# Resident second matrices for the first experts, a direct path for the first queries, and a masked row maximum on VectorE

## The chip, the cores and the metric

The kernel runs on one core of a Trainium2 chip. The metric is the device time of one execution in microseconds (us). TensorE (PE in the rows; PEld is its weight load) multiplies, VectorE (DVE) and ScalarE (ACT) work elementwise, GpSimd (POOL) helps and issues indirect DMAs, and SyncE (SP) issues most of the DMAs. A "q" behind an engine's name (SPq, PEldq) means its sequencer.

## What is computed

Two transformer layers over x, shaped (8, 256, 256), float32. Each has a cross attention and a mixture of experts, and each adds to x:

```python
x = x + L0_xattn(layernorm(x), ctx, ctx, mask, Wq, Wk, Wv, Wout, b_out, causal=1)
x = x + L0_ffn(layernorm(x))     # 16 experts, top 2, 256 -> 512 -> 256, relu
x = x + L1_xattn(layernorm(x), ctx, ctx, Wq, bq, Wk, bk, Wv, bv, Wo, bo)
x = x + L1_ffn(layernorm(x))     # 7 experts, top 2, capacity 732, silu gate, 256 -> 1024 -> 256, one shared expert
```

Both attentions have 16 heads of 16 channels. In the first one a score is closed (minus infinity) above the diagonal and where the mask says so, and a row with every score closed gives zero:

```python
scores = einsum('bhqd,bhkd->bhqk', q, k) / sqrt(16)
scores = where(triu(ones, k=1), -inf, scores)
scores = where(mask[:, None], -inf, scores)
attn = nan_to_zero(softmax(scores))
out = einsum('bhqk,bhkd->bhqd', attn, v)
```

## The kernel before

The work goes stage by stage: first attention, router, first experts, second attention, router, second experts. Semaphores order the engines inside a stage, and all engines meet at a stage's end.

**Attention** (`attend_block`, for both layers). A batch is one of the 8 sequences of 256 rows. Its 16 heads go in four groups of four (G = 4, NG = 4). Queries and keys are cut into three bfloat16 parts each (`split`, lines 320 to 337), whose products are stacked along the contraction dimension in `qs` and `ks`: six rows of 16 channels, so 96 of 104 partitions. To get from a channel-major tile (`parts`) to a stack (16 partitions, heads side by side) the parts go through DRAM: `store_parts` writes them, `load_stack` (lines 133 to 139) reads six pieces. For the first batch's queries `first_queries` (lines 455 to 464) stores each of the three parts as soon as it is cut, and then loads the pieces. All of that is on SP's queue, ahead of the rest of x, `wo`, the third context and the second batch's stacks.

The softmax needs each row's maximum first. `score` (lines 972 to 987) makes scores query-major, `reduce` on VectorE (lines 635 to 639) takes the maxima of a unit, `tops` cuts them in two bfloat16 parts, `turn_tops` turns them, and ScalarE copies them as extra rows into the stack `qs` (line 882). Then `scoreT` makes the scores again, key-major and with the maximum subtracted by the stack's extra rows, ScalarE takes the exponential (line 892), `value` multiplies with the values, and `normalize` divides by the row sums. In the first attention a closed score gets -1e30 added by a second product of the identity with the tile `shut` (lines 986 and 1018). A unit (`UNITS`, line 253) is a PSUM bank full of scores: in the first attention three units per group, one of four heads by 128 keys and two of two heads by 256 keys; two banks take turns (RING = 2), so a unit's scores wait for the reduction of the unit but one before it.

The order on each engine is written out by hand. On TensorE one group is (lines 1110 to 1128): scores of the next group's first unit, turn of this group's maxima, values of the group before, second unit, transposed score of head 0, head 1, third unit, turn of the outputs, heads 2 and 3; between them, by slot (lines 248 to 250), the projections of the batch two ahead and the output projection of the batch before. Batches 6 and 7 have no batch two ahead, so their groups have no such projections. VectorE's group is: the three reductions of the next group, its tops, and the normalization of the group before; in a batch's fourth group also the residual and the statistics of the batch before, and in the first batch the cut of the second queries, the statistics of x and the extra rows of the keys. VectorE's batches run in a loop (`batches`, lines 286 to 293).

**Router** (`route_block`). Norm, logits, top 2 and the lists of which rows go to which expert, mostly on VectorE. In the first layer SP loads the biases `b1` and `b2`, stores the rows and then issues ten loads for the second attention (lines 1262 to 1270).

**First experts** (`experts0_block`). The chosen rows are packed into 47 blocks of 128 rows, each of one expert. For each block SP reads the expert's number and loads both of its matrices (1,024 floats per partition each, 1 MB together) into a ring of four; block n's load waits for block n - 4 to be done. GpSimd gathers the rows, TensorE turns them (`turn`), makes the hidden layer (`first`, line 1713) and the result (`second`, line 1722), ScalarE applies relu, VectorE adds the second bias. TensorE's order is first(j + 1), turn(j + 2), second(j), eleven rounds of four in a loop and three left over.

## Time and profile before

| | us |
|---|---|
| median of 3 runs | 1268.6 (1268.25 to 1268.67) |
| span of the profiled execution | 1262.1 |
| left over for what lies around the span | 6.5 |
| TensorE busy | 1123.7 (89%) |
| VectorE busy | 690.8 (55%) |
| ScalarE busy | 595.9 (47%) |
| GpSimd busy | 360.7 (29%) |

The profiled execution has no time of its own beside its span; the median of the three runs stands for it. The stages lie in the span as follows: first attention 0 to 228 us, router to 262, first experts to about 467, second attention to about 711, router to 736, second experts to the end. Busy time is the union of an engine's instructions; matmuls are pipelined, so a matmul's duration (0.22 us, say) is longer than the step from one to the next (0.06 us), and the starts tell the pace. An idle time in square brackets stands before the row's first instruction, with what ended it. The granted TensorE clock is given as a share of 2.4 GHz.

### The profile page before, as it was taken

The numbers are of one execution on the slowest core, as the hardware profiler recorded it, in microseconds if no ns is written. First come the engines' busy times: TensorE is split into PE (matmuls) and PEld (weight loads), VectorE is DVE, ScalarE is ACT, GpSimd is POOL, SyncE is SP. The second block draws the span as 40 slices with busy tenths as digits, with TensorE's granted clock in tenths as the row PEclk, the third lists the DMA queues.
The fourth block names the chain that finished last, engine by engine and source line by source line (L and its number), as shares of the span: only waits on it lengthen the run. The fifth ranks groups of instructions, "written<-read, shape, count | busy, mean of one in ns | idle before, by whom it ended". The sixth has DMA issues, their size and how long they took to land. (4 is left out here: it accounts for less than half of the span.)

```text
span 1262.1 us, 25941 instructions
## 1 busy us (share of the span) xinstructions
PE 1123.7 (89%) x8539; PEld 974.6 (77%) x8539; DVE 690.8 (55%) x1558; ACT 595.9 (47%) x1211; POOL 360.7 (29%) x502
## 2 busy tenths in 40 slices
PE   5999998739999984888998679999999999999997
PEld 4788786329888873555665379999999999999996
DVE  4755666652222226676767655555556555555556
ACT  3566666313222222776787334444445444444432
POOL 6566650112222205776630145000000000000261
PEclk8899999859999996999999879999999999999999
DMA  7774461548999957568471221223232232232132
GB/s 182 175 180 120 129 179 37 193 159 292 332 330 325 314 207 163 111 136 146 89 125 24 100 89 59 79 63 112 72 103 76 87 109 87 86 100 73 50 97 80
DMA packets 88137, 172.56 MB, mean 137 GB/s; under 512 B 11251, under 2 KB 59949, under 8 KB 81792
## 3 DMA queue, kind: packets, MB, share of 16 engines
q1 hardware_dynamic: 71712, 136.15, 39.0%
q0 software_dynamic: 9584, 29.32, 7.9%
q10 hardware_dynamic: 6768, 6.16, 1.4%
q8 instruction: 40, 0.66, 0.2%
q14 instruction: 33, 0.27, 0.1%
HBM read 133.11 MB, written 39.20 MB: 137 GB/s over the span
## 5 line engine op out<-in xcount | busy, mean ns | idle before, releaser
L2136 PE MATMUL e_ps<-xT_e,wp_e 128*128 128x384 f32 (+1 forms) x1344 | 245.2, 331 | 4.0 <-DVE wp_e L2010 4.0
L2136 PEld LDWEIGHTS e_ps<-xT_e,wp_e 128*128 128x128 f32 x1344 | 221.7, 188 | 5.4 <-issue 4.1
L639 DVE TENSOR_REDUCE att_ps<-att_ps 128x2 f32<-128x512 f32 (+1 forms) x224 | 155.3, 697 | 103.5 <-PE att_ps L986 63.2
L1968 ACT ACTIVATE act_a_e<-e_ps 128x256 f32<-128x256 f32 (+2 forms) x176 | 77.8, 442 | 159.9 <-PE e_ps L2136 150.9
L2066 DVE TENSOR_TENSOR hid_e<-act_a_e,e_ps 128x256 f32<-128x256 f32 (+2 forms) x176 | 87.0, 494 | 116.6 <-ACT act_a_e L1968 102.4
L892 ACT ACTIVATE probs<-att_ps 128x384 f32<-128x384 f32 (+1 forms) x256 | 130.4, 546 | 41.4 <-PE att_ps L1018 29.0
L1972 ACT ACTIVATE hidp_e<-hid_e 128x256 fp32r<-128x256 f32 (+2 forms) x176 | 83.8, 476 | 127.3 <-DVE hid_e L2066 121.5
L2153 PE MATMUL e_ps<-wp_e,hidp_e 128*128 128x256 f32 (+1 forms) x1008 | 138.4, 282 | 2.9 <-DVE xres L2026 1.2
L2068 DVE TENSOR_TENSOR hidp_e<-hid_e,hidp_e 128x256 fp32r<-128x256 f32 (+2 forms) x176 | 87.8, 499 | 95.5 <-ACT hidp_e L1972 90.1
L2153 PEld LDWEIGHTS e_ps<-wp_e,hidp_e 128*128 128x128 f32 (+1 forms) x1008 | 130.7, 183 | 4.9 <-issue 4.1
L1608 ACT ACTIVATE hid_e<-e_ps,b_ahead 128x128 f32<-128x128 f32 x188 | 53.7, 368 | 139.9 <-PE e_ps L1713 129.2
L1919 POOL DMA_DIRECT2D done<-y_e x7 | 6.2, 893 | 384.3 <-DVE y_e L2050 384.3
L984 PE MATMUL att_ps<-ks,qs 96*128 96x256 bf16 (+1 forms) x512 | 102.4, 267 | 11.4 <-DMA qs<-parts 9.5
L2136 PE MATMUL e_ps<-xT_e,swp_e 128*128 128x256 f32 x768 | 106.0, 289 | 1.5 <-issue 0.8
L1016 PE MATMUL att_ps<-qs,ks 104*128 104x256 bf16 (+1 forms) x512 | 99.7, 262 | 3.4 <-ACT qs L882 1.5
L1713 PEld LDWEIGHTS e_ps<-xT_e,w_e 128*128 128x128 f32 x752 | 89.9, 194 | 16.5 <-issue 15.3
L2136 PEld LDWEIGHTS e_ps<-xT_e,swp_e 128*128 128x128 f32 x768 | 98.5, 195 | 2.8 <-DVE swp_e L2005 2.3
L1713 PE MATMUL e_ps<-xT_e,w_e 128*128 128x128 f32 x752 | 94.4, 279 | 6.4 <-DMA w_e<-in_W 5.8
L1589 POOL DMA_INDIRECT x_e<-rows,owner_e x47 | 44.7, 952 | 168.7 <-PE e_ps L1703 125.1
L882 ACT ACTIVATE qs<-att_ps 8x1024 bf16<-8x1024 f32 x64 | 65.1, 1017 | 52.9 <-PE att_ps L997 52.0
L1722 PE MATMUL e_ps<-w_e,hid_e 128*128 128x256 f32 x376 | 88.9, 380 | 0.0
L984 PEld LDWEIGHTS att_ps<-ks,qs 96*128 96x128 bf16 x512 | 48.0, 100 | 39.7 <-issue 20.7
(235 smaller groups left out, 1850.0 us busy)
## 6 DMA issues: line engine op xcount, KB each, us to landing
w_e<-in_W SPq DMA_DIRECT2D x47, 1024.0 KB
w_e<-in_W SPq DMA_DIRECT2D x57, 384.0 KB, 3.1
ks<-parts SPq DMA_DIRECT2D x96, 128.0 KB, 4.7
qs<-parts SPq DMA_DIRECT2D x96, 128.0 KB, 5.2
parts<-cut SPq DMA_DIRECT2D x30, 384.0 KB, 3.2
x_e<-rows SPq DMA_DIRECT2D x8, 768.0 KB, 5.6
done<-y_e ACTq DMA_DIRECT2D x47, 128.0 KB
rows<-zeros POOLq DMA_DIRECT2D x8, 736.5 KB, 6.6
```

Source lines behind the costliest of these rows:

```text
L639: dve.tensor_reduce(tops_at(at[3])[:, qt, x0:x0 + heads], src, AX.X, ALU.max).then_inc(reduced, 1)
L892: act.activation(probs[:, g % 2, x0, 0:WIDE], ps[:, TB + x0 % RING, 0:WIDE], ACT.Exp, scale=DK ** -0.5).then_inc(exped, 1)
L984: last = pe.matmul(out, qs[0:KS, j, hd, qt * P:(qt + 1) * P], ks[0:KS, j, hd, 0:keys(qt)], start=True, stop=not causal)
L1016: last = pe.matmul(out, ks[:, j, hd, kt * P:(kt + 1) * P], qs[:, j, hd, q0:S], start=True, stop=not causal)
L1713: last = pe.matmul(ps[:, HB + j % 2, f * P:(f + 1) * P], w1(j, c, f), xT[:, j % 2, c, :], start=c == 0, stop=c == DC - 1)
L1722: last = pe.matmul(ps[:, YB + j % 2, 0:D], hid[:, j % 2, f, :], w2(j, f), start=f == 0, stop=f == FC0 - 1)
L1968: act.activation(act_a[:, u % 2, 0:n], ps[:, AB + u % 2, 0:n], ACT.Silu).then_inc(silu_ready, 1)
L1972: act.activation(hidp[:, u % 2, 0, 0:n], hid[:, u % 2, 0:n], ACT.Copy).then_inc(hid_high, 1)
L2066: dve.tensor_tensor(hid[:, u % 2, 0:n], act_a[:, u % 2, 0:n], ps[:, BB + u % 2, 0:n], ALU.mult).then_inc(mixed, 1)
L2068: dve.tensor_tensor(hidp[:, u % 2, 1, 0:n], hid[:, u % 2, 0:n], hidp[:, u % 2, 0, 0:n].bitcast(F32), ALU.subtract).then_inc(hid_cut, 1)
L2136: last = pe.matmul(ps[:, bank + u % 2, 0:n], weights(lot, c, pw)[:, (b * DC + d) * P:(b * DC + d + 1) * P], xT[:, px, d, t0:t0 + n], start ...
L2153: last = pe.matmul(out, hidp[:, u % 2, px, t * P:t * P + rows], weights(lot, c, pw)[:, 2 * DC * P:], start=c == 0 and q == 0 and tile % 2 ...
```

## The change

1. First experts: the second matrices of all 16 experts are loaded once, into a tile `w2` of 64 KB per partition, in four loads issued in the router stage. A block's load brings the first matrix alone. TensorE reads the expert's number for each block and takes its second matrix by it. The ten loads for the second attention move from the router stage to the experts' stage, between the loads of blocks 43 and 44.
2. Both attentions: the first batch's queries go from `parts` straight into the stack, in twelve pieces of 64 KB, six issued by SP and six by ScalarE.
3. First attention: `score` leaves out the mask products. `reduce` adds the mask and takes the maximum for each head in one instruction (eight per group), writes the closed scores to a scratch tile and the maxima to SBUF instead of PSUM. VectorE's batches are written out instead of looped. The wait for `shut` moves from `score` to `reduce` and `scoreT`.

```diff
@@ first queries
+        def first_queries(eng, c):
+            for part in range(PARTS):
+                eng.wait_ge(piece_ready if part < PARTS - 1 else parts_ready[0], part + 1 if part < PARTS - 1 else 1)
+                for r in range(len(STACK_Q)):
+                    if STACK_Q[r] == part:
+                        eng.dma_start(qs[r * DK:(r + 1) * DK, 0, c * HPC:(c + 1) * HPC], parts[:, 0, KINDS.index(0), part, c]).then_inc(first_loaded[c], 16)
...
             store_and_load(0, 0, 1)
-            first_queries()
+            first_queries(sp, 0)
...
+            for loaded in first_loaded:
+                sp.wait_ge(loaded, 16 * len(STACK_Q))
+            lead(sp, parts_stored[0], 16)
+            lead(sp, stacks_loaded[0], 16 * len(STACK_Q))
...
                 take_whole(f, f, 0)
+                if f == 0 and ye is not None:
+                    first_queries(act, 1)
                 if f == 0:
                     square_root(1, 1 if ye is not None else NORM - 1, 2)
+                if f == 0 and ye is None:
+                    first_queries(act, 1)
                 if ye is None:
                     take_values(f)
@@ masked maxima
+        row_tops = sb("row_tops", [P, 2, TPB, G])
+            closed_scores = sb("closed_scores", [P, TPB, G, S], BF16)
...
-            return ps[:, MB, (g % 2) * TPB * G:(g % 2 + 1) * TPB * G].rearrange("p (t x) -> p t x", t=TPB)
+            return row_tops[:, g % 2]
...
                 dve.wait_ge(scored, ready(group(at) * NU + u))
+                if causal:
+                    if at[3] == 0 and u == 0:
+                        dve.wait_ge(shut_ready, at[0] + 1)
+                    for x1 in range(heads):
+                        col = x1 * 512 // heads
+                        last = dve.tensor_tensor_reduce(out=closed_scores[:, qt, x0 + x1, 0:keys(qt)], in0=ps[:, unit_bank(at, u), col:col + keys(qt)],
+                                                        in1=shut[:, 0, at[0], qt, 0:keys(qt)], scale=1.0, scalar=MASKED, op0=ALU.add, op1=ALU.max,
+                                                        accum_out=tops_at(at[3])[:, qt, x0 + x1:x0 + x1 + 1])
+                    last.then_inc(reduced, 1)
+                    return
...
-            batches(dve, batch)
+            if causal:
+                for n in range(B):
+                    batch(n, n % 2, n // 2, n == 0, n == B - 1)
+            else:
+                batches(dve, batch)
...
                 if g == 0 and u == 0:
-                    pe.wait_ge(stacks_loaded[j], 16 * len(STACK_Q) * 2 * (r + 1))
-                    if causal:
-                        pe.wait_ge(shut_ready, n + 1)
+                    if isinstance(n, int) and n == 0:
+                        pe.wait_ge(stacks_loaded[j], 16 * len(STACK_K))
+                        for loaded in first_loaded:
+                            pe.wait_ge(loaded, 16 * len(STACK_Q))
+                    else:
+                        pe.wait_ge(stacks_loaded[j], 16 * len(STACK_Q) * 2 * (r + 1))
...
-                    last = pe.matmul(out, qs[0:KS, j, hd, qt * P:(qt + 1) * P], ks[0:KS, j, hd, 0:keys(qt)], start=True, stop=not causal)
-                    if causal:
-                        last = pe.matmul(out, m["identb"][:], closed(n, 0, qt, 0, keys(qt)), start=False, stop=True)
+                    last = pe.matmul(out, qs[0:KS, j, hd, qt * P:(qt + 1) * P], ks[0:KS, j, hd, 0:keys(qt)], start=True, stop=True)
...
+                if x0 == 0 and g == 0 and causal:
+                    pe.wait_ge(shut_ready, n + 1)
@@ first experts
-W0 = DC * F0 + FC0 * D
+W0 = DC * F0
+W2_LOADS = 4
...
-                loaded = ahead["loaded"]
-                for name in ("Wk", "Wv", "Wq", "Wo"):
...
+                w2_sb, w2_loaded = w2
+                for e in range(0, E0, E0 // W2_LOADS):
+                    some = slice(e, e + E0 // W2_LOADS)
+                    sp.dma_start(w2_sb[:, some], a["W2_0"][:, some]).then_inc(w2_loaded, 16)
...
-        def w2(j, f):
-            return w[:, j, DC * F0 + f * D:DC * F0 + (f + 1) * D]
+        def w2(e, f):
+            return w2_sb[:, bass.ds(e, 1), f * D:(f + 1) * D].rearrange("p a d -> p (a d)")
...
-                sp.dma_start(w[:, j], a["W_0"][bass.ds(e, 1)].rearrange("a p f -> p (a f)")).then_inc(w_loaded[j], 16)
+                sp.dma_start(w[:, j], a["W1_0"][bass.ds(e, 1)].rearrange("a p f -> p (a f)")).then_inc(w_loaded[j], 16)
...
             with sp.Fori(0, ROUNDS) as i:
                 for j in range(RING):
                     load(i, j)
+            loaded = ahead["loaded"]
+            for name in ("Wk", "Wv", "Wq", "Wo"):
...
             for j in range(LEFT):
                 load(ROUNDS, j)
...
+            def expert(i, j):
+                return pe.value_load(m["block_expert"][0:1, bass.ds(RING * i + j, 1)], min_val=0, max_val=E0 - 1)
+
-            def second(i, j):
+            def second(i, j, e):
...
                 for j in range(min(known, RING)):
+                    e = expert(i, j)
                     if j + 1 < known:
                         first(*at(i, j + 1))
                     if j + 2 < known:
                         turn(*at(i, j + 2))
-                    second(i, j)
+                    second(i, j, e)
...
             first(0, 0)
+            pe.wait_ge(w2_loaded, 16 * W2_LOADS)
             with pe.Fori(0, ROUNDS) as i:
```

## Rows read from the trace of the kernel before

**Rows 1.** Table of windows; columns: busy (count) per engine, granted clock, DMA share, GB/s.
```profile
31.00:58.00 27.00, 25.50 (x230) 19.23 (x228) 20.85 (x62) 14.37 (x27) 11.86 (x29) 0.86 0.81 186
58.00:180.00 122.00, 121.31 (x1250) 98.54 (x1249) 70.24 (x190) 82.74 (x156) 78.01 (x73) 1.00 0.57 141
...
285.00:461.00 176.00, 169.59 (x1146) 152.80 (x1145) 37.40 (x88) 50.31 (x176) 37.93 (x41) 1.00 0.93 319
```

**Rows 2.** Turns of the maxima (line 997), 58 to 182 us: two per group.
```profile
L997 PE MATMUL att_ps<-identb,top_parts x42: 219/219/220, 58.8 to 180.4; 128*8 128x128 bf16 x42
```

**Rows 3.** Timeline of TensorE, first experts: the first product of four blocks.
```profile
289.11 1.95 PE L1713 MATMUL e_ps<-xT_e,w_e 128*128 128x128 f32 x16
...
292.84 1.95 PE L1713 MATMUL e_ps<-xT_e,w_e 128*128 128x128 f32 x16
...
304.84 2.02 PE L1713 MATMUL e_ps<-xT_e,w_e 128*128 128x128 f32 x16 [0.64 <-DMA w_e<-in_W]
...
461.37 1.95 PE L1713 MATMUL e_ps<-xT_e,w_e 128*128 128x128 f32 x16
```

**Rows 4.** Timeline of SP's queue, router stage: the first load for the second attention.
```profile
237.11 0.60 SPq L1264 DMA_DIRECT2D wk_ahead<-in_Wk  x1
```

**Rows 5.** SP's reads of the expert's number (line 1573); ns minimum/median/maximum.
```profile
L1573 SPq FUSED_REGOPS  x80: 37/152/178, 262.5 to 450.3; - x80
L1573 SPq TENSOR_LOAD <-block_expert x47: 263/268/473, 261.9 to 450.0; - x47
```

**Rows 6.** TensorE's sequencer at line 1709 between 286.25 and 288 us.
```profile
L1709 PEldq ALU_OP  x1: 32/32/32, 286.3 to 286.3; - x1
```

**Rows 7.** Timeline of a steady group in the first attention, TensorE.
```profile
118.64 0.22 PE L986 MATMUL att_ps<-shut,identb 128*128 x1
...
118.69 0.22 PE L984 MATMUL att_ps<-ks,qs 96*128 96x128 bf16 x1
...
120.11 0.28 PE L986 MATMUL att_ps<-shut,identb 128*128 x1
...
120.23 0.27 PE L984 MATMUL att_ps<-ks,qs 96*128 96x256 bf16 x1
...
120.52 0.10 PEld L1016 LDWEIGHTS att_ps<-qs,ks 104*128 104x128 bf16 x1 [0.19 <-ACT qs L882]
```

**Rows 8.** Groups by line and form, VectorE, whole span: busy us, mean ns.
```profile
L639 DVE TENSOR_REDUCE att_ps<-att_ps 128x2 f32<-128x512 f32 x192 | 133.2, 697 | 77.4 <-PE att_ps L986 37.1 <-PE att_ps L984 35.9 <-issue 1.3
...
L1676 DVE TENSOR_TENSOR y_e<-e_ps,b_ahead 128x256 f32<-128x256 f32 x47 | 20.0, 425 | 65.5 <-PE e_ps L1722 65.5
...
L664 DVE TENSOR_TENSOR on<-att_ps,share 128x128 f32<-128x128 f32 x64 | 18.7, 292 | 5.0 <-issue 0.3
```

**Rows 9.** Timeline in the first attention's tail, VectorE and the turn of maxima.
```profile
199.97 0.17 DVE L649 SCALAR_TENSOR_TENSOR top_parts<-att_ps,top_parts 128x8 bf16<-128x8 f32 x1
...
200.19 0.27 PE L997 MATMUL att_ps<-identb,top_parts 128*8 128x128 bf16 x2 [0.24 <-DVE top_parts L649]
...
201.35 1.29 DVE L639 TENSOR_REDUCE att_ps<-att_ps 128x4 f32<-128x512 f32 x2
```

**Rows 10.** Waits, 90 to 200 us: us in total, times, longest.
```profile
DVE att_ps L639 <- PE att_ps L986: 38.4, 47, 2.1
```

**Rows 11.** Timeline of the first attention's start.
```profile
17.84 1.48 SPq L460 DMA_DIRECT2D parts<-cut  x3
...
23.09 2.65 SPq L139 DMA_DIRECT2D qs<-parts  x6
...
26.41 0.60 ACT L846 ACTIVATE vals<-att_ps 128x512 f32<-128x512 f32 x1 [1.61 <-PE att_ps L967]
...
30.67 0.27 PE L984 MATMUL att_ps<-ks,qs 96*128 96x128 bf16 x1 [4.30 <-DMA qs<-parts]
```

**Rows 12.** Timeline of the second attention's start, TensorE.
```profile
498.63 1.09 PE L941 MATMUL att_ps<-ident,h 128*128 128x128 f32 x4 [9.89 <-ACT h L819]
...
500.73 1.01 PE L984 MATMUL att_ps<-ks,qs 96*128 96x256 bf16 x4 [1.02 <-issue]
```

More of the change, by code:

```diff
@@ L221, in attend_block @@
         wq_loaded, wk_loaded, wv_loaded = sem("wq_loaded"), sem("wk_loaded"), sem("wv_loaded")
[L222 removed]
+        v_cleared, piece_ready, first_loaded = sem("v_cleared"), sem("piece_ready"), sems("first_loaded")
         x_loaded, ctx_loaded, flags_loaded = sems("x_loaded", 3), sems("ctx_loaded"), sems("flags_loaded")
@@ L453, in store_and_load @@
                 load_stack(sp, stacks[w], f, parts_dram, w, f, stacks_loaded[f])
-            def first_queries():
-                for part in range(PARTS):
-                    sp.wait_ge(piece_ready if part < PARTS - 1 else parts_ready[0], part + 1 if part < PARTS - 1 else 1)
-                    dst = parts_dram[0, 0, part].rearrange("c p s -> p c s")
-                    sp.dma_start(dst, parts[:, 0, KINDS.index(0), part]).then_inc(pieces_stored[part], 16)
-                for part in range(PARTS):
-                    sp.wait_ge(pieces_stored[part], 16)
-                    load_stack(sp, qs, 0, parts_dram, 0, 0, stacks_loaded[0], (part,))
-                sp.sem_inc(parts_stored[0], 16)
             if ye is not None:
@@ L1177, in _, with route_block @@
                 project(B - 1, t)
-def route_block(nc, m, layer, E, a, hall, router, shared=None, biases=None, rows=None, W=None, ctxT=None, ahead=None):
+def route_block(nc, m, layer, E, a, hall, router, shared=None, biases=None, rows=None, w2=None):
     ctx = ExitStack()
@@ L1510, in _, with experts0_block @@
                 dve.tensor_copy(m["block_expert"][:], owner[:])
-def experts0_block(nc, m, a, rows, ye, b1, b2, b_loaded):
+def experts0_block(nc, m, a, rows, ye, b1, b2, b_loaded, w2_sb, w2_loaded, W, ahead):
     ctx = ExitStack()
@@ L1579, in _ @@
                     load(i, j)
+            loaded = ahead["loaded"]
+            for name in ("Wk", "Wv", "Wq", "Wo"):
+                sp.dma_start(ahead[name.lower()][:], W[name].rearrange("(c p) n -> p c n", p=P)).then_inc(loaded, 16)
+            for at_w, name in enumerate(("bq", "bk")):
+                sp.dma_start(ahead["bias"][:, at_w], W[name].rearrange("(c p) -> p c", p=P), allow_slow_non_contiguous=True).then_inc(loaded, 16)
+            for name in ("bo", "bv"):
+                sp.dma_start(ahead["bo" if name == "bo" else "bvb"][:], W[name].partition_broadcast(P)).then_inc(loaded, 16)
+            for j in range(2):
+                sp.dma_start(ahead["cst"][:, j], a["ctxT"].rearrange("(c p) t -> p c t", p=P)[:, :, j * S:(j + 1) * S]).then_inc(loaded, 16)
             for j in range(LEFT):
@@ L1721, in second @@
                 for f in range(FC0):
-                    last = pe.matmul(ps[:, YB + j % 2, 0:D], hid[:, j % 2, f, :], w2(j, f), start=f == 0, stop=f == FC0 - 1)
+                    last = pe.matmul(ps[:, YB + j % 2, 0:D], hid[:, j % 2, f, :], w2(e, f), start=f == 0, stop=f == FC0 - 1)
                 last.then_inc(y_made, 1)
```

20 lines of the change are left out of this document (6 added, 14 removed).

## Prediction, made before any run of the change

> **What bounds the kernel now.** The changed places lie in the first 711 us of the span; the last 526 us are the second experts, which the change leaves alone. I read the stages in the table of windows first [rows 1]. In the first attention's steady part (58 to 180 us) TensorE is busy 121.3 of 122 us at full clock, VectorE 70.2: TensorE's work sets the pace, and a group of four heads takes (180.4 - 58.8) / 20 = 6.08 us [rows 2]. In the first experts (285 to 461 us) TensorE and DMA are both near full: 169.6 of 176 us and a DMA share of 0.93. Which of the two ends last is seen block by block. While weights are in store, a block takes 292.84 - 289.11 = 3.73 us; later TensorE waits for a landing, as for the 0.64 us ahead of 304.84 [rows 3]. The 43 periods from 289.11 to 461.37 (the last block's) take 172.3 us; TensorE alone would need 43 x 3.73 = 160.4. So 11.9 us there belong to the weights' transfers.
>
> **First experts: second matrices resident.** A block's load falls from 1,048 KB to 524 KB. With 131 KB of rows in and 131 KB of results out a block moved 1.31 MB in 172.3 / 43 = 4.0 us (319 GB/s in the window of rows 1); it will move 0.79 MB in 3.73 us, or 211 GB/s. Two thirds of the measured rate: the wait goes, and TensorE's own 3.73 us is late next. Gain: 11.9 us. The resident 8.4 MB are issued where the loads for the second attention stood, at 237.11 [rows 4]. At 319 GB/s they take 26 us, to 263, just as the first loads for the experts are issued; four small loads behind them on SP's queue (2.1 MB, 7 us) are in by 270. TensorE needs them three blocks ahead of 289.11, near 278. The first block's first product also runs ahead of the new wait for the second matrices. Hidden by the router stage and the listing of rows, with 8 us of cover left. If the rate were a third lower, the first block would start about 5 us late. The ten loads for the second attention, taken from the router stage, now stand on SP between the loads of blocks 43 and 44: 1.8 MB, some 6 us of transfer, and ten issues of about 0.5 us. Block 44's load was due 4 blocks (15 us) ahead of its use, so it lands in time; I allow 0.4 us. The second attention starts some 20 us after these issues.
>
> TensorE gets a new step per block: it reads the expert's number from SBUF into a register. On SP's queue such a load takes 268 ns and its register arithmetic 152 ns [rows 5]. No row shows it on TensorE. Its sequencer, however, runs far ahead of the array: it passes the wait of the first product of the next block (line 1709) at 286.3 us [rows 6], while that product starts at 289.11 [rows 3], 2.8 us later. About 0.6 us of sequencer work is then covered: nothing, my choice. Uncovered it would cost at most 0.6 us in each of 47 blocks, 28 us. *First experts: 11.9 - 0.4 = 11.5 us gained.*
>
> **First attention, TensorE.** The mask product behind each score product goes. A 128-column product starts 0.05 to 0.06 us after the one before it (118.64, 118.69), a 256-column one 0.12 us (120.11, 120.23) [rows 7]. Per group four of each go: 4 x 0.057 + 4 x 0.112 = 0.68 us. Not all is gained. The masks of the group's second unit (0.22 us) lie between the turn of the maxima and the first transposed score, and there TensorE already waits 0.19 us for ScalarE's row copy (120.52) [rows 7]; that wait only grows. 0.46 us per group are on the path.
>
> **First attention, VectorE.** Three reductions of 697 ns per group become eight fused add-and-maximum instructions, four over 128 and four over 256 elements. No row shows such an instruction. The nearest with one input in PSUM: 292 ns over 128, 425 ns over 256 [rows 8]. Back to back, two reductions take 1.29 us, so each follower hides 0.10 us of itself [rows 9]; the eight would take 4 x 0.19 + 4 x 0.32 = 2.04 us if the maximum came out for nothing. The maximum must still be written out. The nearest row is an operation over 8 elements, 0.17 us (199.97) [rows 9]. Lower bound: it hides 0.10 us of itself too, 0.07 each; upper bound: nothing overlaps. Sums: 2.04 + 8 x 0.07 = 2.6 us, and 4 x (0.292 + 0.425) + 8 x 0.17 = 4.2 us. I take 3.25 us, nearer the lower end, since operations that don't depend on each other do overlap in rows 9, though the write-out depends on its main. Against 3 x 0.697 = 2.09 us that is 1.15 us more per group, between 0.5 and 2.1.
>
> In 90 to 200 us VectorE waited 38.4 us for score products [rows 10], in 19 groups: 2.0 us per group. TensorE's gain takes 0.46 of it, so 1.55 remain for 1.15: hidden on average. In the fourth group of a batch VectorE also has the residual and the statistics; I allow 0.5 us there over five batches. Twenty steady groups: 20 x 0.46 - 0.5 = 8.7 us gained. The tail has no such cover: at 200.19 TensorE waits for the maxima, and at 201.35 reductions run back to back [rows 9]. Of its eight groups I let two pay 1.0 us each, three 0.25, and three gain 0.3: 1.9 us lost (8 x 1.15 = 9 at most). The new wait for the masks on TensorE is met long before. VectorE's loop written out costs only instruction fetch; I take nothing, at most 1 us.
>
> **First queries.** In the first attention the third cut's store is the last of three issued from 17.84 on, and the stack loads follow at 23.09, when the stores have landed; TensorE starts scoring at 30.67, having waited 4.30 us for them [rows 11]. Moved straight, SP issues six pieces from 17.84 on, in the 2.65 us that six loads take now, to 20.5; the other six stand on ScalarE's queue, and behind them the copy of the first values, then the second batch's keys and rows. That chain held ScalarE until 27.01 (the copy at 26.41) and moves by about 1.1 us, to 28.1. This, not the landing (the loads now take at most 30.67 - 25.74 = 4.9 us after their last issue, so 25.4), is late next: 2.5 us gained, or 2.2 at the first maxima. But the first batch's groups also hold the cuts of the second queries and the statistics of six batches on VectorE, with little idle time, and 4 x 1.15 less 4 x 0.46 is 2.8 us. I put the first batch with its head start at nothing, from 1.5 lost to 3 gained; the upper end is there because the clock of 0.86 in 31 to 58 us [rows 1] follows TensorE's idle time, which shrinks. In the second attention the rows of the second batch are turned from 498.63 to 499.7 and scoring begins at 500.73 [rows 12]: 1.0 us gained, and no more, since the turning is late next. ScalarE waits there for the last cut with its six issues, but its next work follows the second batch's rows, just ahead of 498.63. SP's later stores and loads come 3 to 5 us earlier in both; no row shows who would gain.
>
> **The sum**: 11.5 + 8.7 - 1.9 + 0 + 1.0 = 19.3 us. The profiled span is 1262.1 us, the median 1268.6; the 6.5 us around the span stay. I predict 1268.6 - 19.3 = 1249.3 us.
>
> **Rivals.** (A) The write-out of the maximum is not overlapped, 4.2 us per group. VectorE then bounds the steady groups too: 2.1 against 2.0 us of idle time, 2 us lost instead of 8.7 gained; the other twelve groups, for which I allow 0.9 us of idle time, lose 12 x 1.2 = 14 us less the 2.2 of the start. With the 12.5 us gained elsewhere this gives 1268.6 + 2 + 12 - 12.5 = 1270 us. For it: the write-out needs its main's result. Against it: the overlap in rows 9. The Trainium skill, page "VectorE: DVE Perf Modes", section "Two Vector instructions with no wait between them", counts an operation with an accumulator output as two instructions; the same page, section on the TRN2 errata, says that many small tiles pay a fixed latency each and advises tiles of 512 elements or more. Both speak against this edit; its formula for PSUM sources, (120 + elements) / 0.96 GHz, would give 258 and 392 ns, so 2.6 us for the eight mains alone, an estimate from that page, where rows 8 give 2.9 with nothing overlapped.
> (B) Slower: the fused instruction runs at half the element rate. Its place is the eight instructions of each group, its price 4 x 0.133 + 4 x 0.267 = 1.6 us more, so 4.8 us per group and 2.8 over now. It decides from 2.1 us over (A's end). Then 20 x 0.8 + 12 x 1.9 - 2.2 = 37 us are lost and 12.5 gained: 1293 us. Against it: every two-input row in the trace runs at one element per cycle.
> (C) TensorE's register load is not covered: 28 us, 1277 us. Against it: rows 6. The skill's page "DMA: Bandwidth & Descriptors", section "Latency and other measured facts", gives a floor of about 600 ns for such a load; the 268 ns of rows 5 lie below, and at that floor with no cover the sum would be the same 1277.
> (D) More is gained: with the write-out at its lower bound the tail (1.9) and the fourth groups (0.5) lose nothing, and the first batch gains its 3: 1243.9 us. For it: 0.5 us over lies under every idle time named.
> (E) The straight move starts no score earlier, because values and keys are late anyway: 3 us less, 1253.
>
> **Chances.** The forecast 0.55, A 0.13, B 0.05, C 0.04, D 0.10, E 0.08, something else slower 0.05. The range, 1243 to 1270, reaches over D, E and A. About 0.2% (2.5 us) is what a measurement of this kernel can tell from no change. A lies at that edge and is split 0.03, 0.07, 0.03; so faster 0.76, same 0.07, slower 0.17.
>
> **What would show it.** Block periods of 3.73 us throughout 285 to 450 us and no wait for weights; gaps ahead of line 1713's first loads would mean C. Group periods near 5.6 us in the steady part; TensorE waiting for the top parts (line 649) in most groups would mean A or B. Durations of the fused rows, and their spacing, settle 3.25 us. Scoring should begin near 28 and, in the second attention, about 1 us after its turning less than now. The prediction is wrong if VectorE's reductions take over 4 us per group, or if the expert stage keeps 4.0 us per block.

## The result and the profile after

The changed kernel takes 1260.55 us in the median of five runs (1255.55 to 1262.43). The ratio to the kernel before is 0.9926, 95% interval 0.9903 to 0.9949: 9.4 us less by the ratio (6.5 to 12.3), 8.05 by the medians. The forecast was 19.3. The sign and the range held, but less than half of the gain came.

The head of the page of the changed kernel, and its table of windows (columns as in [rows 1]):

```profile
span 1257.7 us, 26159 instructions
...
PE 1105.0 (88%) x8283; PEld 958.1 (76%) x8284; DVE 723.9 (58%) x1974; ACT 595.8 (47%) x1211; POOL 361.7 (29%) x502
```

```profile
31.00:58.00 27.00, 22.53 (x191) 16.30 (x190) 22.58 (x119) 14.91 (x28) 9.26 (x24) 0.87 0.66 150
58.00:180.00 122.00, 113.08 (x1085) 86.44 (x1082) 89.07 (x444) 83.11 (x157) 80.81 (x78) 0.97 0.58 141
...
285.00:461.00 176.00, 172.95 (x1184) 162.31 (x1182) 39.06 (x92) 52.40 (x184) 38.83 (x41) 0.99 0.67 204
```

Against [rows 1], the experts' window shows what was meant: DMA share 0.67 for 0.93, TensorE at its own pace. The steady attention (second line) does not show it: TensorE has 8 us less work and as much more idle time, so nothing was gained in it. (It idles in the first batches too, 4.5 us of 27 where it idled 1.5.) The profiled execution took 1259.55 us for a span of 1257.7. So 1.85 us lie around the span, not the 6.5 that I read off before; the profiled execution of the kernel before was one of its short ones (about 1264), which matters for one term below.

The stages of all profiles in one table, us, each read off one profiled execution. "Start": from the end of the first queries' last cut to the turn of the maxima of group 4. "Steady": the 20 groups to group 24. "Tail": the next 7. "Experts": first to last product of the first experts. "Gap": from there to the second attention's first score. "Second": first to last turn of maxima there. The last column is the ratio to the kernel before, with its interval, and comes from all runs. The kernels are those of the next section.

| kernel | start | steady | tail | experts | gap | second | ratio |
|---|---|---|---|---|---|---|---|
| before | 41.0 | 121.5 | 34.0 | 187.8 | 34.2 | 179.9 | 1 |
| before_sbuf | 40.3 | 122.9 | 33.8 | 191.5 | 34.6 | 183.4 | 1.0064 (1.0042 to 1.0087) |
| part1_only | 40.0 | 121.5 | 34.5 | 180.9 | 33.8 | 179.2 | 0.9913 (0.9889 to 0.9938) |
| part2_only | 41.5 | 124.0 | 33.8 | 192.5 | 34.3 | 180.5 | 1.0051 (1.0028 to 1.0074) |
| part2_signal | 40.6 | 121.5 | 35.0 | 194.0 | 33.1 | 183.0 | 0.9995 (0.9970 to 1.0020) |
| part3_only | 40.5 | 117.2 | 31.6 | 193.2 | 34.2 | 184.3 | 0.9997 (0.9974 to 1.0019) |
| part3_psum | 42.9 | 113.7 | 33.7 | 192.1 | 33.5 | 181.0 | 0.9941 (0.9917 to 0.9964) |
| changed | 40.8 | 122.4 | 32.5 | 180.1 | 32.8 | 185.4 | 0.9926 (0.9903 to 0.9949) |
| tops_psum | 41.2 | 119.2 | 33.6 | 180.0 | 33.4 | 181.9 | 0.9924 (0.9894 to 0.9955) |
| signal_early | 38.6 | 120.1 | 32.0 | 180.2 | 33.8 | 182.4 | 0.9889 (0.9856 to 0.9922) |
| ahead_last | 40.6 | 124.2 | 31.5 | 176.3 | 33.0 | 189.2 | 0.9915 (0.9886 to 0.9943) |
| three | 40.5 | 114.0 | 33.7 | 176.3 | 33.1 | 180.3 | 0.9804 (0.9776 to 0.9831) |
| three_without2 | 42.2 | 115.3 | 34.3 | 176.0 | 33.4 | 178.9 | 0.9832 (0.9801 to 0.9862) |
| three_all_sp | 37.7 | 115.1 | 34.2 | 176.3 | 32.5 | 180.1 | 0.9821 (0.9792 to 0.9851) |

What one profile can tell: where the code of a stage is the same, the steady part took 121.5 us three times, but the experts with the old weights 187.8 to 194.0 us in six profiles, and the second attention with its maxima in PSUM 178.9 to 183.0 us in nine. A difference of 2 or 3 us in one profile's "experts" or "second" shows nothing by itself.

**Three losses in the trace of the changed kernel.** First, VectorE by form, 90 to 180 us (busy us, mean ns, idle time before):

```profile
L647 DVE CUSTOM_DVE_ANT_0 closed_scores<-att_ps,shut 128x256 bf16<-128x256 f32 x62 | 23.8, 421 | 12.6 <-PE att_ps L1009 12.1
L647 DVE CUSTOM_DVE_ANT_0 closed_scores<-att_ps,shut 128x128 bf16<-128x128 f32 x60 | 13.8, 286 | 2.6 <-PE att_ps L1009 2.5
L663 DVE SCALAR_TENSOR_TENSOR top_parts<-row_tops,top_parts 128x8 bf16<-128x8 f32 x16 | 10.5, 657 | 1.2
L647 DVE DVE_READ_ACCUMULATOR2_ANT row_tops<- 128x1 f32 x122 | 10.1, 83 | 0.0
L661 DVE TENSOR_SCALAR top_parts<-row_tops 128x8 bf16<-128x8 f32 x16 | 7.6, 476 | 1.8 <-issue 0.4
```

The fused instructions are as quick as hoped. What stands out are two instructions that the diff doesn't touch: the cuts of the maxima (`tops`), 8 elements each. They took 0.17 us [rows 9], and now take 0.66 and 0.48 in the mean. The timeline shows on what:

```profile
120.27 1.27 POOL L532 TENSOR_TENSOR xres<-xres,bo 128x512 f32<-128x512 f32 x1
...
120.42 1.15 DVE L663 SCALAR_TENSOR_TENSOR top_parts<-row_tops,top_parts 128x8 bf16<-128x8 f32 x1
...
125.95 1.16 POOL L332 TENSOR_TENSOR rest<-full,cut 128x512 f32<-128x512 f32 x1
125.97 1.17 DVE L661 TENSOR_SCALAR top_parts<-row_tops 128x8 bf16<-128x8 f32 x1
```

The VectorE instruction ends when the GpSimd instruction ends (121.57 against 121.54; 127.14 against 127.11). In the whole trace 32 of the 128 cuts take over 0.3 us, and 31 of them end within 0.15 us of a GpSimd instruction's end; in the trace of before none takes over 0.17. The excess is 14.3 us in the steady part and 10.0 in the second attention, which the prediction took to change at its start only and whose turns now take 185.4 us for 179.9. The line that places the maxima, `tops_at`, serves both attentions, although the change is listed under the first one. What changed for these two instructions is their source: `row_tops` in SBUF for PSUM. The Trainium skill, page "SBUF — State Buffer", section "Who interferes with whom", has a rule for this: VectorE and GpSimd share a pair of SBUF ports as an exclusive lock; VectorE needs it when it has two SBUF inputs and GpSimd reads SBUF, or when it runs in a 2-port mode; and the one that issues second waits until the other's whole instruction is over. The trace agrees with the waiting: the 31 stretched cuts end with a GpSimd instruction. Line 663 (13 of the 32 long ones) has two SBUF inputs. Line 661 (19 of them) has one, so by the rule it would have to run in a 2-port mode, and no trace here names the mode.

Second, GpSimd's next cut after 31 us, and what TensorE has of it:

```profile
46.22 0.61 POOL L330 CAST cut<-full 128x512 bf16<-128x512 f32 x1 [14.59 <-SPq L145]
```

```profile
78.57 0.60 PE L1009 MATMUL att_ps<-ks,qs 96*128 96x128 bf16 x4 [2.97 <-DMA qs<-parts]
```

Line 145 is `lead`: SP's signal that the first batch's parts may be overwritten. In the kernel before it followed the first queries' loads, at 25.8 us; now it stands behind the whole of the second batch's stores and loads. GpSimd cuts the third batch's keys at 46.2 for 41.4 us, their store and stacks follow late, and TensorE waits for the stacks: from the turn of group 6 to that of group 7 it took 9.61 us, where the kernel before takes 6.73.

Third, the first experts near block 44, TensorE's timeline:

```profile
439.45 1.95 PE L1742 MATMUL e_ps<-xT_e,w_e 128*128 128x128 f32 x16
...
445.22 2.60 PE L1742 MATMUL e_ps<-xT_e,w_e 128*128 128x128 f32 x16 [1.88 <-DMA w_e<-in_W]
```

From the third block on every block period is 3.73 us but two. Taken at a block's first product, as in [rows 3], they are 5.77 and 5.47 us; taken at the first product of the second matrix, 6.59 and 4.66. They belong to the first blocks whose weights were issued behind the ten loads for the second attention. Either way 3.8 us are lost where 0.4 was allowed. SP's queue shows the larger half of the cause:

```profile
428.59 4.07 SPq L1595 DMA_DIRECT2D w_e<-in_W  x2
432.87 0.40 SPq L1602 DMA_DIRECT2D wk_ahead<-in_Wk  x1
...
437.44 0.94 SPq L1608 DMA_DIRECT2D cst_ahead<-in_ctxT  x2
439.16 4.70 SPq L1595 DMA_DIRECT2D w_e<-in_W  x3
```

In the rounds before, a block's load is issued 3.73 us after the last one and 7.13 us ahead of its first product. Block 43's is issued at 432.32, so block 44's was due at 436.05; the ten issues hold the queue until 438.4, and it goes out at 439.16, 3.1 us late.

### The profile page after: what moved, and what is told of

Read it like the earlier page. It is cut to its first block and busy times, and to the rows that moved or that the text cites. A ratio compares the mean times of both kernels' runs of the same rounds, so it can differ in the third digit from the quotient of the medians.

```text
span 1257.7 us, 26159 instructions
## 1 busy us (share of the span) xinstructions
PE 1105.0 (88%) x8283; PEld 958.1 (76%) x8284; DVE 723.9 (58%) x1974; ACT 595.8 (47%) x1211; POOL 361.7 (29%) x502
## 5 line engine op out<-in xcount | busy, mean ns | idle before, releaser
L653 DVE TENSOR_REDUCE row_tops<-att_ps 128x2 f32<-128x512 f32 x128 | 87.5, 687 | 33.8 <-PE att_ps L1009 29.8
L647 DVE CUSTOM_DVE_ANT_0 closed_scores<-att_ps,shut 128x128 bf16<-128x128 f32 (+1 forms) x256 | 77.2, 353 | 38.5 <-PE att_ps L1009 37.4
L1009 PE MATMUL att_ps<-ks,qs 96*128 96x256 bf16 (+1 forms) x512 | 88.4, 266 | 9.6 <-DMA qs<-parts 5.2
L1742 PEld LDWEIGHTS e_ps<-xT_e,w_e 128*128 128x128 f32 x752 | 93.2, 196 | 4.5 <-issue 2.2
L1618 POOL DMA_INDIRECT x_e<-rows,owner_e x47 | 44.7, 951 | 160.2 <-PE e_ps L1732 115.1
L1754 PE MATMUL e_ps<-w_ahead,hid_e 128*128 x376 | 89.7, 382 | 0.0
```

The costliest lines, as they stand in the source:

```text
L653: dve.tensor_reduce(tops_at(at[3])[:, qt, x0:x0 + heads], src, AX.X, ALU.max).then_inc(reduced, 1)
L1009: last = pe.matmul(out, qs[0:KS, j, hd, qt * P:(qt + 1) * P], ks[0:KS, j, hd, 0:keys(qt)], start=True, stop=True)
L1742: last = pe.matmul(ps[:, HB + j % 2, f * P:(f + 1) * P], w1(j, c, f), xT[:, j % 2, c, :], start=c == 0, stop=c == DC - 1)
L1754: last = pe.matmul(ps[:, YB + j % 2, 0:D], hid[:, j % 2, f, :], w2(e, f), start=f == 0, stop=f == FC0 - 1)
```

## Experiments

**Each loss mended alone, and the first one put into the kernel before.** `tops_psum` is the changed kernel with

```diff
-            return row_tops[:, g % 2]
+            return ps[:, MB, (g % 2) * TPB * G:(g % 2 + 1) * TPB * G].rearrange("p (t x) -> p t x", t=TPB)
```

> The changed kernel, with the row maxima written to PSUM again, in both attentions; nothing else differs. Theory P (SBUF port): in the changed kernel 31 of the 128 small VectorE instructions that cut the maxima (167 to 172 ns otherwise) take 0.6 to 2.1 us and end when a GpSimd instruction ends; 14.3 us of such excess lie in 58 to 180 us and 10.0 us in the second attention. With their source in PSUM they are all back at about 167 ns, the second attention's groups go back to their length before (about 5.5 us less), the first attention's steady groups gain about 0.25 us each (5 us), and the time falls by 8 to 11 us, to about 1251. Theory V (VectorE has too many instructions): the fused instructions and their accumulator reads are what delays TensorE; then the first attention stays as it is (turns of the maxima from 58.2 to 180.6 us) and the time falls by at most 5.5 us, if at all, to 1255 to 1261.

Measured: 1256.53 us, ratio 0.9924. By the ratio that can't be told from the changed kernel; by the medians it is 4 us less. The 8 to 11 us expected did not come. The stages say in part why. All 128 cuts are short:

```profile
L662 DVE SCALAR_TENSOR_TENSOR top_parts<-att_ps,top_parts x64: 165/167/168, 34.2 to 676.9; 128x8 bf16<-128x8 f32 x64
```

and the second attention gives 3.5 us back (181.9 for 185.4). But in the steady part only 3.2 us come: from the turn of group 6 to that of group 7 it takes 10.5 us now for 9.6. TensorE is ahead, and waits longer for the late stacks. The two stages give 6.7 us in this one profile, where the ratio has 0.3, so more of the gain stays unaccounted for.

`before_sbuf` is the kernel before with the same line changed the other way.

> The kernel before, with only the row maxima's place changed from PSUM to SBUF (both attentions; the three reductions a group stay as they were). Theory P (SBUF port): the two cutting instructions now wait for GpSimd's instructions; some 25 to 35 of them are stretched to the end of a GpSimd instruction, the second attention gets about 5.5 us longer as it did in the changed kernel, the first attention 1 to 6 us, and the time rises to about 1277 (1274 to 1281). Theory V (number of instructions): the place of the maxima costs nothing, 1268.6.

Measured: 1276.54 us, 1.0064 (1.0042 to 1.0087), 8.1 us slower (5.3 to 11.0). This isolates the cause: not one instruction more, only the maxima's place. The cuts, ns minimum/median/maximum:

```profile
L650 DVE SCALAR_TENSOR_TENSOR top_parts<-row_tops,top_parts x64: 166/168/2111, 36.9 to 701.4; 128x8 bf16<-128x8 f32 x64
L648 DVE TENSOR_SCALAR top_parts<-row_tops x64: 170/173/2079, 36.7 to 700.8; 128x8 bf16<-128x8 f32 x64
```

37 of 128 are stretched, by 28.9 us in all; 35 of them end with a GpSimd instruction. Theory P holds, V falls. The control is `tops_psum`: there 49 of the 128 cuts start while a GpSimd instruction on SBUF has more than 0.17 us to go, and none is stretched. (The profile's stages show 3.5 us in the second attention and 1.4 in the steady part; the rest of the 8.1 isn't found in that one profile, whose other stages differ by as much from run to run.)

`signal_early` is the changed kernel with the wait and the two signals moved:

```diff
-            store_and_load(1, 0, 1)
+            store(1, 0, 1)
+            for loaded in first_loaded:
+                sp.wait_ge(loaded, 16 * len(STACK_Q))
+            lead(sp, parts_stored[0], 16)
+            lead(sp, stacks_loaded[0], 16 * len(STACK_Q))
+            sp.wait_ge(parts_stored[1], 16)
+            load_stack(sp, stacks[1], 1, parts_dram, 1, 1, stacks_loaded[1])
```

> The changed kernel, with SP's wait for the first queries' pieces and its two signals moved ahead of the second batch's stack loads, where SP waits for a store anyway. Theory S (late signal): GpSimd's cut of the third batch's keys waited 14.6 us for the signal that SP now gives at 46.1 us, and TensorE lost 5.2 us in groups 6 and 7 to the third batch's stacks. With the signal at about 28 us GpSimd cuts from 32 us on, the stall shrinks to under 1.5 us, and the time falls by 3 to 5 us, to about 1256.5. Rival (crowded transfers): the third batch's stacks are late because the straight pieces fill the queues; then the stall stays and the time stays at 1260.5.

Measured: 1253.93 us, 0.9889: 4.7 us less than the changed kernel by the ratios, 6.6 by the medians. GpSimd's cut:

```profile
40.13 0.61 POOL L330 CAST cut<-full 128x512 bf16<-128x512 f32 x1 [7.59 <-ACT full L860]
```

It no longer waits for SP but for ScalarE's copy of the keys, which I had overlooked when I wrote "from 32 us on": the signal had cost 6 us there, not 14. From the turn of group 6 to that of group 7 it takes 6.6 us. So the stall that theory S names is gone. The time alone would not settle it, since the two ratios' intervals overlap; `part2_only` and `part2_signal` below do.

`ahead_last` is the changed kernel with the ten loads behind the last block's load:

```diff
+            for j in range(LEFT):
+                load(ROUNDS, j)
             loaded = ahead["loaded"]
...
-            for j in range(LEFT):
-                load(ROUNDS, j)
```

> The changed kernel, with the ten loads for the second attention issued behind the last block's load instead of between the loads of blocks 43 and 44. Theory A (in the way): the 3.8 us that blocks 44 and 45 lost (periods 6.59 and 4.66 us instead of 3.73) come from their weights landing behind those 1.8 MB; all periods are then 3.73 us or less and the time falls by 3.8 us, to about 1256.8. Rival (the end of the blocks is slow anyway, or the loads are then late for the second attention): the second attention's first score does not move against the end of the first experts by less than it gains, and the time stays within 1 us of 1260.5.

Measured: 1259.21 us, 0.9915, in the direction of theory A but not to be told from no change. The stage is plain: from the third block on all periods are 3.73 us, the experts take 176.3 us for 180.1, and the second attention's first score follows as closely as before (33.0 for 32.8). In its profile the second attention then took 189.2 us, with groups of 9.3 and 9.0 us. The profiled execution was the longest of its six (1266.79 us), and `three` has the same loads in the same place and takes 180.3, so the loads are hardly to blame.

Why were the weights late? `part1_only`, which has the ten loads in the same place, shows both halves. Block 44's load goes out at 443.02 us, 3.4 us after it was due, and lands at 449.05, 0.23 us ahead of its first product. That is 6.0 us after its issue, where the median of the 47 is 4.1. So the ten issues on SP's queue made it 3.4 us late and the crowded transfers some 2 us more, against 2.4 to 3.0 us that the loads of the blocks before landed early.

**All three together, and the parts alone.** `three` holds all three mends.

> The changed kernel with all three mends: the maxima in PSUM, SP's signal ahead of the second batch's stack loads, the ten loads behind the last block's load. Measured alone against 1260.5 us they gave 4.0, 6.6 and 1.3 us. Theory T (they hide each other's gain): with the maxima in PSUM alone the gain of the first batches ran into a longer wait for the third batch's stacks (periods of 10.5 us in the first and 9.9 us in the second attention, where 6.3 and 5.9 are the rule), so together they give more than their sum of 11.9: 5 + 9 + 3.7 = 17 to 18 us, to about 1243. Rival I (they overlap: each removes the same wait): together no more than the largest, 6.6 to 8 us, 1253.

Measured: 1243.72 us, 0.9804 (0.9776 to 0.9831), 24.9 us less than before and 15.5 less than the changed kernel by the ratios, where the mends alone sum to 0.3 + 4.7 + 1.4 = 6.4. Rival I falls: it allowed 1253 us, and the slowest of six runs took 1246.35. Theory T has the time right. That the losses hid each other is seen in the traces at one place, the wait for the third batch's stacks, which grew from 9.6 to 10.5 us in `tops_psum`; the 9.1 us between 15.5 and 6.4 are no more than the intervals of the four ratios leave open. The windows (the same columns; stages end earlier here):

```profile
58.00:180.00 122.00, 117.26 (x1172) 90.22 (x1170) 90.35 (x490) 89.11 (x169) 80.35 (x78) 1.00 0.64 158
285.00:448.00 163.00, 163.00 (x1130) 153.60 (x1128) 36.55 (x87) 49.72 (x175) 36.63 (x39) 1.00 0.71 211
```

In the experts TensorE has no idle time left. The steady part takes 114.0 us for 121.5.

`part1_only`, `part2_only` and `part3_only` are the kernel before with one part of the diff each.

> The kernel before with the first part alone: second matrices resident, the ten loads between the loads of blocks 43 and 44. From the first product to the last of the first experts the kernel before took 187.8 and 191.5 us in two profiles, the changed one 180.1. Theory 1 (the weights' transfers were the wait, and the ten loads give 3.8 us back): 8 to 11 us less, 1258 to 1260, which is all that the whole change brought. Rival: the register load on TensorE or the four loads in the router stage take some of it; less than 5 us gained, above 1263.

Measured: 1257.93 us, 0.9913, 11.0 us less (7.9 to 14.1). As expected.

> The kernel before with the second part alone: the first queries straight into the stacks, and with it the late signal of SP. Theory S: scoring starts about 1.2 us earlier in the first and 1 us in the second attention, but GpSimd's cut of the third batch's keys waits for the signal at about 46 us and TensorE for the stacks; slower by 2 to 5 us, about 1271.5. Rival: it gains what the start gains, 1 to 3 us, about 1266.

Measured: 1275.81 us, 1.0051 (1.0028 to 1.0074), 6.5 us more: the part that was to gain cost more than even theory S said.

> The kernel before with the third part alone: VectorE masks and takes the maxima per head, the maxima go to SBUF. Theory P: the mask products' 0.46 us per group are gained (8 to 9 us over the first attention), the small instructions that wait for GpSimd's lose 8.5 us over both attentions, as the same move cost the kernel before; sum about zero, 1266 to 1270. Rival V (the eight instructions lose on their own): 1272 or more.

Measured: 1268.23 us, 0.9997: 0.4 us less (2.4 more to 3.3 less), as theory P says: the steady part gains 4.3 us, the tail 2.4, and the second attention loses 4.4.

The same parts with their own mend (`part3_psum`: the line of `tops_psum`; `part2_signal`: the lines of `signal_early`):

> The kernel before with the third part alone, and the maxima left in PSUM. Theory P: without the small instructions' waits for GpSimd the third part gives what the mask products took. In the kernel with all three mends twenty steady groups took 114.1 us against 121.6 before, so 7.5 us are gained there, and the last seven groups and the second attention stay as they were: 7 to 8.5 us less, about 1261. Rival V (the masked maxima cost VectorE more than the mend shows): gain under 4 us, 1265 or more.

Measured: 1259.86 us, 0.9941, 7.5 us less (4.6 to 10.5). Its profile has 7.8 us of gain in the steady part, 113.7 for 121.5; the other stages differ by what one profile can't tell from nothing.

> The kernel before with the second part alone and SP's signal early. Theory S: the 6 us that the second part alone cost were the late signal; with it early the time is that of the kernel before or 1 us less (1267.5 to 1268.5), since scoring starts only about 0.5 us earlier in the first attention and 0.8 in the second. Rival (the straight pieces themselves cost something, through ScalarE's six issues or the longer transfers): 1271 or more.

Measured: 1268.33 us, 0.9995 (0.9970 to 1.0020), 7.1 us less than `part2_only`, with intervals that don't meet. The signal was all that the second part cost, and with the signal early the part brings nothing that can be measured here. The profiles of `part2_only` and `part2_signal` show 3.4 us of the 7 (start and steady); where the others lie they don't show.

**What the straight move is worth in the mended kernel.** `three_without2` leaves the second part out of `three`; `three_all_sp` lets SP issue all twelve pieces:

```diff
             first_queries(sp, 0)
+            first_queries(sp, 1)
...
-                    first_queries(act, 1)
```

> The kernel with all three mends, without the second part: the first queries go through DRAM as before. Theory S: the straight pieces gain at most 1.3 us over both attentions, so this one takes 1243.7 to 1245. Rival: in this kernel, where TensorE is ahead of the stacks, the straight way gains the 2.2 and 1.0 us that were forecast for it: 1247.

Measured: 1247.57 us, 0.9832. Its interval (0.9801 to 0.9862) overlaps with that of `three`; the value is the rival's. Some 3.5 us for the straight move are possible there, not shown.

> The kernel with all three mends, with all twelve straight pieces issued by SP, none by ScalarE. Theory L (landing): a 64 KB piece takes about 7 us from issue to landing, twice what a 128 KB load from DRAM took, and the last landing sets the first score; with all on SP the last issue comes about 3.5 us later, scoring starts 2 to 4 us later in both attentions, 1247 to 1250. Rival C (ScalarE's six issues hold back the first values, keys and rows): scoring starts no later, the first batch gains up to 1 us, 1243.

Measured: 1245.87 us, 0.9821, again not to be told from `three`. Neither theory is right as it stands, and the timelines show what sets the first score. ScalarE and TensorE in the changed kernel:

```profile
15.31 3.92 ACTq L365 DMA_DIRECT2D qs<-cut  x6
19.28 0.60 ACT L864 ACTIVATE vals<-att_ps 128x512 f32<-128x512 f32 x1 [4.79 <-issue]
...
28.64 0.60 ACT L864 ACTIVATE vals<-att_ps 128x512 f32<-128x512 f32 x1 [1.13 <-PE att_ps L989]
```

```profile
21.39 1.12 PE L963 MATMUL att_ps<-ident,h 128*128 128x128 f32 x4 [5.40 <-ACT h L837]
...
29.44 0.60 PE L1009 MATMUL att_ps<-ks,qs 96*128 96x128 bf16 x6 [0.84 <-issue]
```

and ScalarE in `three_all_sp`:

```profile
19.21 0.60 ACT L866 ACTIVATE vals<-att_ps 128x512 f32<-128x512 f32 x1 [1.05 <-PE att_ps L987]
...
29.36 0.60 ACT L866 ACTIVATE vals<-att_ps 128x512 f32<-128x512 f32 x1 [1.24 <-PE att_ps L987]
```

In the kernel before TensorE waited 4.30 us for the stacks [rows 11]. In the changed kernel that wait is gone, and the first score comes 0.8 us after the start of ScalarE's second copy of values; so it does in all seven profiles with six issues on ScalarE, in which the last straight piece had landed 1.5 to 4.7 us ahead of the score. There the landing (theory L) is not the bound; ScalarE's chain is. With six issues on it the copy comes 11.3 us after the last cut of the queries (17.35) in the changed kernel, without them 8.3 us in `three_all_sp` (21.02), and the score follows 9.1 us after that cut, for 12.1 to 13.4 us in the seven. Theory L's 2 to 4 us later did not come. But the landing is no longer far: here too the profile puts the score down to ScalarE's copy,

```profile
30.16 0.60 PE L1007 MATMUL att_ps<-ks,qs 96*128 96x128 bf16 x6 [0.84 <-ACT vals L866]
```

while the last piece landed at 29.84, 0.32 us ahead of it; in the six profiles that load the queries through DRAM the score follows the last landing by 0.24 to 0.35 us. So in `three_all_sp` both end together. The start is 37.7 us, for 38.6 to 41.5 in the seven. That gain doesn't show in the median, and where it goes is open.

## Why the prediction was right in sign and wrong in size

Most of the gains that the sum counts are there; it failed at three costs that it put at nothing or too low. The change of the maxima's memory was costed for VectorE's writing alone, and cost 8.1 us in their reading. The first queries' move was costed by its transfers alone, and the signal behind it cost 6.5 us. And "it lands in time; I allow 0.4 us" for block 44's weights was 3.8 us. With the three removed the kernel gains 24.9 us.

**First experts, 11.5 us: right, by two errors that cancel.** Part 1 alone gave 11.0. All the rest of its case held: periods of 3.73 us, TensorE's register load hidden (rival C falls), the resident matrices in time, and from the route's start to the first product 51.0 to 52.0 us in eight profiles with them against 50.2 to 51.9 in six without. TensorE's load of the expert's number into a register, for which the prediction had no row, takes 0.30 us there (median of 47). But the ten loads cost 3.8 us, not 0.4. The step that failed: "Block 44's load was due 4 blocks (15 us) ahead of its use, so it lands in time". The traces show a load issued 7.1 us ahead of its use, landed some 4.1 us later, with under 3 us to spare. The ten issues took 3.1 to 3.4 us of that, and the transfers some 2 us more. And the 11.9 us of [rows 3] were low, most likely because the profiled execution was a short one. The experts took 187.8 us in it and 191.5 to 194.0 in the five other profiles with the old weights. By the mean of the six the gain is 192 - 176.3 = some 16 us, less 3.8.

**First attention, TensorE, 0.46 us per group: somewhat high.** With the cuts undisturbed and the signal early, twenty groups gain 6.2 to 7.8 us in four profiles (`three_without2` 115.3, `three_all_sp` 115.1, `three` 114.0, `part3_psum` 113.7, for 121.5), 0.3 to 0.4 each; 8.7 were forecast.

**VectorE, 3.25 us per group: too high, even its lower bound.** The fused instructions of the changed kernel, back to back:

```profile
122.40 0.08 DVE L647 DVE_READ_ACCUMULATOR2_ANT row_tops<- 128x1 f32 x1
122.40 0.29 DVE L647 CUSTOM_DVE_ANT_0 closed_scores<-att_ps,shut 128x128 bf16<-128x128 f32 x1
122.61 0.08 DVE L647 DVE_READ_ACCUMULATOR2_ANT row_tops<- 128x1 f32 x1
...
123.04 0.42 DVE L647 CUSTOM_DVE_ANT_0 closed_scores<-att_ps,shut 128x256 bf16<-128x256 f32 x1
123.38 0.08 DVE L647 DVE_READ_ACCUMULATOR2_ANT row_tops<- 128x1 f32 x1
123.38 0.42 DVE L647 CUSTOM_DVE_ANT_0 closed_scores<-att_ps,shut 128x256 bf16<-128x256 f32 x1
```

The write-out of the maximum is an instruction of its own, 83 ns, and starts together with the next main. One head takes 0.21 us over 128 and 0.34 us over 256 elements: 4 x 0.21 + 4 x 0.34 = 2.2 us per group, against 2.09 before. Rivals A and B fall. The write-out is nearly hidden: the spacing is 0.02 us above the 0.19 and 0.32 us that the prediction worked out for mains without one. The durations, 286 and 421 ns, are close to the 292 and 425 of [rows 8] and above the 258 and 392 of rival A's formula. The tail's 1.9 us of loss did not come either: 33.7 us in `three` and `part3_psum` for 34.0.

**The step that failed for the first attention** is one that the working does not have: a cost put at nothing without a word. It follows the maxima's place to the instruction that writes them and not to the two that read them, and takes those over at 0.17 us [rows 9]. Their source went to SBUF, and there they wait for GpSimd's instructions: 8.1 us alone (`before_sbuf`), 7.1 between `part3_only` and `part3_psum`, and the second attention, for which only a start was counted, pays 4.4 us of it (180.5 us in the mean of the nine profiles with PSUM maxima, 178.9 to 183.0; 184.9 in the five with SBUF, 182.4 to 189.2). The prediction asked what the new instructions cost VectorE by themselves, and not what another engine does in the memory that they now read.

**First queries: the wait that moved.** "SP's later stores and loads come 3 to 5 us earlier in both; no row shows who would gain" looked at the DMAs of the queue and not at its signals. A signal that GpSimd waits for went 20 us later (25.8 to 46.1). Alone it cost 6.5 us (7.1 between `part2_only` and `part2_signal`), where the range for the first batch allowed 1.5 lost. And ScalarE's chain, which "moves by about 1.1 us", moved by 2.8 from the last cut on (26.41 - 17.88 = 8.5; 28.64 - 17.35 = 11.3): six issues cost it 3.9 us. Rival E was nearly right: from the last cut to the first score 12.1 us for 12.8, 0.7 gained for 2.5; in the means of seven profiles with the six issues on ScalarE and six with the way through DRAM it is 12.7 for 13.1. The clock that was to rise there with less idle time stayed, 0.87 for 0.86 in 31 to 58 us, with more idle time. The second attention's start gained 0.7 us in the mean of the gaps (33.3 in eight profiles with the second part, 34.0 in six without) for 1.0.

**The sum.** By the parts alone: -11.0 + 6.5 - 0.4 = -4.9 us; measured -9.4 (6.5 to 12.3 less). Each part's interval is about 3 us to either side, so the two agree, and losses that hide each other would pull the same way. With the three mends the kernel takes 24.9 us less than before, more than the 19.3 forecast: the three costs together took 15.5 us.

## What to carry to other kernels

When a buffer changes its memory, cost the instructions that read it too, and look at which other engine is busy in SBUF while they run: eight elements can take 2 us. When a step is moved on a queue, list the signals that it gives as well as its DMAs, and find who waits for each; and ask of loads slipped in between others what stands behind them, counting the issues as well as the bytes, from the lead time that the trace shows. Read a stage's length off more than one execution before taking a transfer-bound wait as exact; and when two losses sit on one path, mending one of them shows little of what both are worth.

## What the runs showed of the hardware

- A VectorE instruction over 8 elements with its source in SBUF, 0.17 us by itself, took up to 2.13 us beside GpSimd's. With its source in PSUM none of 128 (`tops_psum`) took over 0.168 us. The fused instruction, with one source in PSUM and one in SBUF, is not held up: 74 of its 256 mains in the changed kernel lie wholly within a GpSimd instruction, and none takes over 0.43 us.
- The accumulator's read-out takes 83 ns into SBUF and 140 ns into PSUM (mean of 129, `tops_psum`), and the mains beside it 313 and 441 ns for 286 and 421. So where GpSimd does little the SBUF place looks like the better one: the tail, in which GpSimd is busy 6.5 of 48 us, takes 31.5 to 32.5 us in the four profiles with the fused instructions and SBUF maxima, and 33.6 to 34.3 in the five with those in PSUM.
- Twelve loads from SBUF to SBUF of 64 KB, six each on SP's and ScalarE's queue, took 7.0 us from issue to landing in the first attention of the changed kernel (median; 5.5 to 7.6). All twelve on SP's queue (`three_all_sp`) took 3.4 us (2.5 to 4.8). Their issue took 0.60 us on SP and 0.62 us on ScalarE, against 0.42 for a stack's load from DRAM.
- A load of 524 KB, issued behind ten others (1.8 MB), took 6.0 us to land, where the median of its kind is 4.1 us (`part1_only`).
- The start of an execution has two forms: the last cut of the first queries ends at 17.3 to 18.3 us in seven profiles and at 20.7 to 21.0 in the other seven, one profile per kernel. Both forms occur among kernels whose start is the same code (`before` and `part1_only`), so this is likely 3 us of the spread between executions; one profile per kernel can't show it.
